# An adaLN transformer block with grouped attention and routed experts on one core: projections and attention rewritten, with unrolled halves, one key tile at a time, and q and k stored once

## The reference

```python
mod = (silu(c) @ wmod).reshape(4, 6, 1, 256)      # sa, ca, ga, sb, cb, gb; |ga|, |gb| at least 0.25
h = layernorm(x) * (1 + ca) + sa                  # x: (4, 512, 256)
q, k, v = h @ wq, h @ wk, h @ wv                  # 32 query heads, 8 key/value heads, head size 8
att = softmax(causal(q @ k.T / sqrt(8)))          # all in float32
x = x + ga * ((att @ v) @ wo)
h = layernorm(x) * (1 + cb) + sb
scores = softmax(h @ gate_w.T)                    # 16 experts in 4 groups; 2 groups, then 4 experts are kept
out = sum over the kept experts of weight * (swiglu(h @ up[e].T) @ down[e].T)
out = out + swiglu(h @ shared_up.T) @ shared_down.T
x = x + gb * out
```

## Time and profile before

| | us |
|---|---|
| median of three unprofiled runs | 829.13 (824.28 to 831.57) |
| span of the profiled execution (its own time; no other is recorded for it) | 853.4 |
| PE busy in it | 669.9 (79%) |
| DVE busy | 472.6 (55%) |
| GpSimd busy | 360.5 (42%) |
| ACT busy | 325.6 (38%) |

### The profile page before, as it was taken

How to read it: one execution, slowest core, us unless ns; L and a number is a source line. 1 busy time by engine, 2 the same in 40 slices (tenths; PEclk the granted TensorE clock), 3 DMA queues, 4 the chain that set the end, 5 groups by cost and what they waited for, 6 DMA issues and landing times.

```text
span 853.4 us, 14386 instructions
## 1 busy us (share of the span) xinstructions
PE 669.9 (79%) x3412; PEld 367.3 (43%) x3413; DVE 472.6 (55%) x921; ACT 325.6 (38%) x752; POOL 360.5 (42%) x441
## 2 busy tenths in 40 slices
PE   1697078999989989998769868435999999999950
PEld 1365033343444444343126436223666566565630
DVE  7496087677859686885357676141333333333326
ACT  1143005675737565573642322011333333333320
POOL 9233114353333534352332574730555455555540
PEclk9999589999999999999677987856999999999995
DMA  5058902141504223220109952332555555555548
GB/s 204 0 168 230 297 26 59 36 120 36 133 21 126 77 70 88 72 77 2 51 3 303 396 153 81 138 136 85 90 90 95 87 96 91 93 89 88 96 49 289
DMA packets 114127, 94.77 MB, mean 111 GB/s; under 512 B 47696, under 2 KB 106032, under 8 KB 114096
## 3 DMA queue, kind: packets, MB, share of 16 engines
q1 hardware_dynamic: 97472, 73.00, 29.4%
q0 software_dynamic: 14448, 19.31, 13.6%
q10 hardware_dynamic: 2176, 2.10, 0.7%
HBM read 47.66 MB, written 44.22 MB: 108 GB/s over the span
## 4 chain that ended last, share of the span: by engine, by line
PE 29%; issue 20%; DVE 12%; DMA 9%; SPq 8%; ACT 5%; POOL 3%; DVEq 1%; POOLq 1%; ACTq 0%
PE bank L812 7%; DMA y_sum<-arena,token_no 7%; PE bank L996 6%; DVE negm L1277 5%; PE bank L802 4%; PE bank L1013 4%; ACT arena L1071 4%; PE bank L784 3%; SPq L724 2%; PE bank L830 2%; DVE arena L544 2%; SPq L725 1%; PE bank L1004 1%; POOL arena L1180 1%; DVE arena L1504 1%
## 5 line engine op out<-in xcount | busy, mean ns | idle before, releaser
L1071 ACT ACTIVATE arena<-bank 128x512 f32<-128x512 f32 x320 | 176.3, 599 | 116.0 <-PE bank L802 112.3
L1277 DVE TENSOR_REDUCE negm<-bank 128x2 f32<-128x1024 f32 (+3 forms) x176 | 190.3, 1116 | 36.8 <-PE bank L788 36.3
L1244 POOL DMA_INDIRECT y_sum<-arena,token_no x79 | 123.0, 1556 | 141.9 <-DVE arena L1509 133.3
L1180 POOL TENSOR_SCALAR_AFFINE_SELECT arena<-arena 128x512 f32<-128x512 f32 x128 | 81.7, 651 | 158.0 <-ACT arena L1071 154.1
L784 PE MATMUL bank<-arena 96*128 96x512 bf16 (+3 forms) x512 | 114.3, 304 | 35.2 <-DVE credits L1263 27.6
L802 PE MATMUL bank<-arena 96*128 96x512 bf16 x320 | 118.7, 400 | 15.4 <-ACT arena L1071 10.8
L996 PE MATMUL bank<-arena 128*128 x316 | 116.2, 491 | 1.1 <-issue 1.1
L1498 DVE CAST token_no<-arena 128x1 uint32<-128x1 f32 x79 | 12.2, 154 | 144.5 <-DMA y_sum<-arena,token_no 133.9
L788 PE MATMUL bank<-mask_qk,ident_bf 128*128 128x128 bf16 (+2 forms) x352 | 87.2, 248 | 0.0
L1235 POOL DMA_INDIRECT x_rows<-arena,slots x64 | 64.2, 1003 | 52.3 <-DVE slots L1410 33.7
L812 PE MATMUL bank<-arena 128*32 128x512 f32 x640 | 79.3, 624 | 6.3 <-POOL arena L1180 6.3
(11 more groups left out here) (174 smaller groups left out, 819.0 us busy)
## 6 DMA issues: line engine op xcount, KB each, us to landing
arena<-x_rows SPq DMA_DIRECT2D x79, 136.5 KB
q_parts<-arena SPq DMA_DIRECT2D x24, 384.0 KB, 3.8
arena<-q_parts SPq DMA_DIRECT2D x32, 288.0 KB
arena<-up_t SPq DMA_DIRECT2D x2, 2816.0 KB
arena<-k_parts SPq DMA_DIRECT2D x16, 288.0 KB
y_parts<-arena SPq DMA_DIRECT2D x64, 64.0 KB
arena<-y_parts SPq DMA_DIRECT2D x16, 256.0 KB, 3.0
arena<-y_sum SPq DMA_DIRECT2D x8, 512.0 KB, 6.9
```

The lines of the kernel that those rows point to most:

```text
L1071: nc.scalar.activation(pool[:, q % 2, g * QT + kt, :], bank[:, buf, :], ACT.Exp, scale=SCALE).then_inc(s["st_free"], 1)
L1180: nc.gpsimd.affine_select(out=block_, in_=block_, compare_op=ALU.is_ge, fill=0.0, base=0, pattern=[[0, REP], [1, P]], channel_multiplier=- ...
L1244: gp.indirect_dma_start(y_sum[i % 2], bass.IndirectOffsetOnAxis(ap=token_no[i % STEPS][:, :], axis=0), yo[i % STEPS], None, compute_op=ALU ...
L1277: nc.vector.tensor_reduce(to, view, AX.X, ALU.max, negate=True).then_inc(s["s_free"], 1)
```

## The change

The two blocks become one, and the halves are written out, u = 0 to 7, with constant counts in all waits. Each part of q and k is stored once (2 stores for each batch), and a load of a half reads them three times, into 24 rows each, for all 512 queries; there are three buffers of `Q` and `K`, and no `K0`. GpSimd clears V and 32 rows of each K, and only behind the first layer norm. PE turns two batches ahead of the projections. The gates are computed once, as 4 rows for the four batches, in the midst of the first maxima, and go through DRAM (`mod_rows`) to all partitions. `GROUPS` orders the score tiles by query tile and key tile, the diagonal one first, and then by g; the exponentials of a group of four go to one of four slots of `probs`, and `weigh_values` runs group by group, where `WEIGH` puts it. The values go out as before, but each total once (`y_totals`); they come back as 128x64, are inverted in one reciprocal, go to DRAM (`y_inverse`) and come back repeated. The last half keeps the old way. The second layer norm starts in the first groups of the last half, the shared expert's weights are loaded ahead of the halves, and the clearing of `y_sum` comes after half 1. Routing, the expert tiles and the end are the same code at other places of `arena`.

```diff
+GROUPS = [(q, kt) for q in range(QT) for kt in (q, *range(q))]
+NG = len(GROUPS)
+E_TOT = NG * GH
+FIRST = {q: GROUPS.index((q, q)) for q in range(QT)}
+S_HEADS = {0: 4, 1: 2, 2: 1, 3: 1}
+S_PAIRS = {q: HH // (2 * S_HEADS[q]) for q in range(QT)}
+S_BASE = {q: sum(S_PAIRS[k] for k in range(q)) for q in range(QT)}
+S_TOT = sum(S_PAIRS.values())
+WEIGH = {1: [(1, 8), (1, 9)], 2: [(0, 0)], 4: [(0, 1), (0, 2)], 6: [(0, 3), (0, 4)], 7: [(0, 5)], 9: [(0, 6), (0, 7)]}
+LEAVE = {1: (1, 3), 2: (0, 0), 4: (0, 1), 7: (0, 2)}
+SLOTS = 4
+QBUF = 3
...
-    q_parts = nc.dram_tensor("q_parts", (B, 2, PARTS, PARTS, HD, HH, T), BF16, kind="Internal").ap()
-    k_parts = nc.dram_tensor("k_parts", (B, 2, PARTS, PARTS, HD, GH, T), BF16, kind="Internal").ap()
+    q_parts = nc.dram_tensor("q_parts", (B, 2, PARTS, HD, HH * T), BF16, kind="Internal").ap()
+    k_parts = nc.dram_tensor("k_parts", (B, PARTS, 2, HD, GH * T), BF16, kind="Internal").ap()
...
-                for h in range(2):
-                    nc.gpsimd.memset(Q[h][:, :, :, :], 0.0)
-                    nc.gpsimd.memset(K[h][:, :, :], 1.0)
-                    last = nc.gpsimd.memset(K0[h][:, :, :], 0.0)
-                last.then_inc(s["cleared_q"], 1)
...
+        def pairs_after(q, slot):
+            n = (q + 1) * GH
+            return range(slot * S_PAIRS[q] // n, (slot + 1) * S_PAIRS[q] // n)
...
+                def store_parts(b):
+                    i = b % 2
+                    sp.wait_ge(s["low_done"], b + 1)
+                    sp.dma_start(q_parts[b].rearrange("h j d (n t) -> (d n) (h j) t", n=HH),
+                                 parts[i][:, 0:2, :, :].rearrange("p h j t -> p (h j) t")).then_inc(q_out[i], 16)
+                    sp.dma_start(k_parts[b].rearrange("j h d (g t) -> (h d g) j t", g=GH),
+                                 parts[i][0:64, 2, :, :]).then_inc(q_out[i], 16)
+                def load_half(u):
+                    b, h, i = u // 2, u % 2, u % QBUF
+                    for n in range(PARTS):
+                        rows_ = slice(PARTS * HD * n, PARTS * HD * n + PARTS * HD)
+                        sp.dma_start(Q[i][rows_, :, :].rearrange("p n t -> p (n t)"),
+                                     q_parts[b, h].rearrange("j d m -> (j d) m")).then_inc(q_in[i], 16)
+                        sp.dma_start(K[i][rows_, :, :].rearrange("p g t -> p (g t)"),
+                                     k_parts[b, n, h].unsqueeze(0).to_broadcast([PARTS, HD, GH * T])).then_inc(k_in[i], 16)
...
+                def fetch_values(u):
+                    h = u % 2
+                    sp.wait_ge(y_out[h], 128 * (u // 2 + 1))
+                    above(sp, s["y_ready"], u)
+                    if u % 2 == 0:
+                        above(sp, s["x2_ready"], u)
+                    sp.dma_start(totals, y_totals[h].rearrange("n (a t) -> (n a) t", a=P // (GH * REP))).then_inc(t_in[h], 16)
+                    sp.dma_start(Yp[0][:, :], y_values[h].rearrange("g r d t -> (g r d) t")).then_inc(y_in[h], 16)
+                def spread_inverse(u):
+                    h = u % 2
+                    sp.wait_ge(s["inverted"], u + 1)
+                    sp.dma_start(y_inverse[h].rearrange("n (a t) -> (n a) t", a=P // (GH * REP)), inverse
+                                 ).then_inc(i_out[h], 16)
+                    sp.wait_ge(i_out[h], 16 * (u // 2 + 1))
+                    sp.dma_start(Yp[1][:, :], y_inverse[h].unsqueeze(1).to_broadcast([GH * REP, HD, T])).then_inc(y_in[h], 16)
...
+                store_parts(0)
+                store_parts(1)
+                sp.wait_ge(q_out[0], 32)
+                sp.wait_ge(s["k_ones"], QBUF)
+                load_half(0)
+                load_half(1)
+                store_parts(2)
+                store_parts(3)
+                sp.wait_ge(q_out[1], 32)
+                load_half(2)
+                sp.wait_ge(s["gate_rows"], 1)
+                sp.dma_start(mod_rows, row_mod[0:B, :, :].rearrange("p m d -> p (m d)")).then_inc(s["gate_out"], 16)
+                sp.wait_ge(s["gate_out"], 16)
+                sp.dma_start(gate_bc[:, :, :, :].rearrange("p b m d -> p (b m d)"),
+                             mod_rows.rearrange("b m -> (b m)").unsqueeze(0).to_broadcast([P, B * 4 * D])
+                             ).then_inc(s["gate_bc"], 16)
...
+                for u in range(HALVES):
+                    if u > 0 and u + 2 < HALVES:
+                        sp.wait_ge(s["st_ready"], E_TOT * u)
+                        if (u + 2) % 2 == 0:
+                            sp.wait_ge(q_out[(u // 2 + 1) % 2], 32 * ((u // 2 + 1) // 2 + 1))
+                        load_half(u + 2)
+                    put_negm(u, QT - 1)
+                    if u > 0:
+                        send_values(u - 1)
+                    if u + 1 < HALVES:
+                        put_negm(u + 1, 0)
+                    if u > 0:
+                        fetch_values(u - 1)
+                    if u + 1 < HALVES:
+                        put_negm(u + 1, 1)
+                    if u > 0:
+                        spread_inverse(u - 1)
+                    if u + 1 < HALVES:
+                        put_negm(u + 1, 2)
...
+                def gate_rows():
+                    pe.wait_ge(s["wg_in"], 16)
+                    for k in range(2):
+                        for c in range(DC):
+                            last = nc.tensor.matmul(bank[0:B, 6 + k, :], sc_sb[:, c, :],
+                                                    wmod_sb[:, c, GA * P + 512 * k:GA * P + 512 * k + 512],
+                                                    start=(c == 0), stop=(c == DC - 1))
+                    last.then_inc(s["gate_mm"], 1)
...
+                def weigh_values(u, n):
+                    b, h, (q, kt) = u // 2, u % 2, GROUPS[n]
+                    pe.wait_ge(s["st_free"], E_TOT * u + GH * n + GH)
+                    if kt == q:
+                        pe.wait_ge(s["p_ready"], GH * (QT * u + q) + GH)
+                        above(pe, s["o_free"], QT * u + q)
+                    for g in range(GH):
+                        last = nc.tensor.matmul(bank[32 * g:32 * g + 32, OBANK, :], V[:, b * QT + kt, h * GH + g, :],
+                                                probs[:, (NG * u + n) % SLOTS, g, :], start=(kt == q),
+                                                stop=(kt == max(q - 1, 0)), skip_group_check=True)
                     last.then_inc(s["av_done"], 1)
...
+                            slot = GH * (n - FIRST[q]) + g
+                            scores(u, n, g)
+                            if g == 0:
+                                for back_, m in WEIGH.get(n, ()):
+                                    if u - back_ >= 0:
+                                        weigh_values(u - back_, m)
+                            if u + 1 < HALVES:
+                                for i in pairs_after(q, slot):
+                                    scores_for_max(u + 1, q, i)
+                            if (n, g) == (0, 2):
+                                turn_max(u, QT - 1)
+                            elif kt == q and g == 2 and u + 1 < HALVES:
+                                turn_max(u + 1, q - 1)
+                            if u % 2 == 0 and u > 0 and (n, g) in ((8, 3), (9, 1)):
+                                project(u // 2 - 1, int(n == 9))
...
+                turn_x(0)
+                turn_x(1)
+                pe.wait_ge(s["w_in"], 48)
+                for b in range(B):
+                    project_in(b)
+                    if b + 2 < B:
+                        turn_x(b + 2)
...
+                    if q == 1:
+                        gate_rows()
+                        pe.wait_ge(s["gate_rows"], 1)
...
+                            tile = E_TOT * u + GH * n + g
+                            act.wait_ge(s["st_ready"], tile + 1)
+                            nc.scalar.activation(probs[:, group % SLOTS, g, :], bank[:, 4 + tile % 2, :], ACT.Exp,
+                                                 scale=SCALE).then_inc(s["st_free"], 1)
+                        if u == HALVES - 1 and n == FIRST[QT - 1]:
+                            deviation2(act, 0, B - 1)
...
+                gp.wait_ge(s["xn_ready"], 1)
+                nc.gpsimd.memset(V, 1.0).then_inc(s["v_ones"], 1)
+                gp.wait_ge(s["v_ones"], 1)
+                for i in range(QBUF):
+                    nc.gpsimd.memset(K[i][64:96, :, :], 1.0).then_inc(s["k_ones"], 1)
+                    gp.wait_ge(s["k_ones"], i + 1)
+                low(0)
...
+                def invert(u):
+                    dve.wait_ge(t_in[u % 2], 16 * (u // 2 + 1))
+                    nc.vector.reciprocal(inverse, totals).then_inc(s["inverted"], 1)
+                def normalise(u):
+                    dve.wait_ge(y_in[u % 2], 32 * (u // 2 + 1))
+                    nc.vector.tensor_tensor(Y[u % 2][:, :], Yp[0][:, :], Yp[1][:, :], ALU.mult).then_inc(s["y_ready"], 1)
...
```

(9 more changed lines are left out.)

993 lines of the change are left out of this document (425 added, 568 removed).

## The result

The changed kernel takes 802.9 us (median of 4 runs, 799.3 to 806.2) where the kernel before, run beside it, takes 830.4 (824.3 to 832.8): ratio 0.9694, 95% interval 0.9641 to 0.9747. It is faster by 27 us; 71 were forecast, and the time lies outside my range. The profiled execution took 799.3 us.

What follows compares the result with a forecast made beforehand. It took the head as bound by clearing and SyncE's serial stores and loads, the halves by DVE behind at q = 3 with PE stalling. Head -43, halves -19, last half -9 sum to -71: 829.1 - 71 = 758 us, range 730 to 788.

Steps and rivals of the forecast that it cites:

- Head: Everything up to the first half's E scores: earlier projections, fewer stores, gates moved; -43 us, from -30 to -50.
- (a): Head: GpSimd clears less, behind the first layer norm; projections start near 18.5 instead of 31.34: -13 us.
- (b): Head: gate matmuls, 3.62 to 3.72 us a batch, leave the projection loop; projections end near 54, was 80.
- (c): Head: fewer stores, first half's data loaded in 5.5 us; first scores near 57 instead of 107.5: -50, between -35 and -55.
- the rule on K's load: Head: K's load, its source repeated 3 times, uses 3 engines: 5.6 us, hidden, or scores 2 to 3 later.
- Step (d): First maxima: gates as rows, PE 3.6 then DVE near 4; +5 us, between 0 and 9; broadcast ends near 81.
- Halves: Attention halves: odd 34, even 38 us, with up to 2 us stall for totals; -19 us, from -5 to -38.
- DVE's 3 us: In each half: one 128x64 reciprocal replaces four of 128x128, 3.5 us becoming about 0.5, -3 on DVE.
- Last half: Last half: early second norm, 36 us to the end of scores instead of 41.4, fewer values behind; -9, 0 to -14.
- Rival (1): Only the head pays; halves bound by PE alternating with ACT and DVE, and by late totals: 781 us, chance 0.17.
- Rival (4): Head gains only 25: 16 KB rows at half rate, loads ahead of later stores and gates; 776 us, chance 0.12.
- Rival (3): Unrolled halves: straight code stalls about 11.5 us in each of 8, 92 in all; 850 us, chance 0.03.

Runs made afterwards that it cites:

- k_rows: The changed kernel with rows of q and k in the order (dimension, part), so K's load has no leading repeat of 3: 776.8 us, ratio 0.9386.
- k_split: The changed kernel with each load of K split into three loads of 8 rows without a repeat, in the old order: ratio 0.9508.
- before_again: The kernel before, unchanged, profiled a second time: span 830.0, time 831.8 us.
- gates_first: The changed kernel with the third half's load behind the gates' rows, their broadcast and the first three minus-max rows in SyncE's queue: 803.6 us, ratio 0.9666.
- invert_late: The changed kernel with DVE's reciprocal of the totals three tiles later in the half: 788.8 us, ratio 0.9505.
- recip_small: The kernel before with each reciprocal on 16 of 128 columns, leaving out part of the result: 826.6 us, ratio 0.9949.
- recip_big: k_rows with twelve more reciprocals of 128x32 a half on DVE: 795.9 us, ratio 0.9624.
- bridge_last: k_rows with gates earlier, third half's load and reciprocal later, and unused matmuls in the last half, ten before the square-root wait: 768.4 us, ratio 0.9276.
- all_six: bridge_last with 22 unused matmuls ahead of the first scores: 765.0 us, ratio 0.9239.
- k_rows_again: k_rows, unchanged, measured again as a reference: 779.0 us, ratio 0.9415.

## Why the prediction was wrong, step by step

**Head, -43 forecast, -28 to -31 measured.** Steps (a), (b) and the stores of (c) held: projections from 19.95 (18.5 forecast) to 53.1 (54), stores at 36.7 and 45.2 (36 and 45), DVE's first `tensor_scalar` 1.38. The term that failed is "the data of the first half at 275 GB/s takes 5.5": the first scores came at 68.1 instead of 57, and 8.0 us of the 11 are the load of K, as k_rows shows and k_split confirms (62.3, with Q's load untouched). The other 3 remain in k_rows (60.1); the wait of 7.16 there is still for K. I had put the rule on K's load into a sentence of its own, with 2 to 3 us estimated by the Trainium skill ("DMA: Bandwidth & Descriptors", section on why a DMA increments its semaphore by 16). Its sign held: with 8 as the slowest dimension the load is faster than with 3, in both forms tried. My price from it was too small, 8.0 at the first scores, and it left out the queue behind the load; no row here shows how many engines a load took. Step (d), the gates, was +5 and is 7.25 (76.05 to 83.30), PE's 3.6 and DVE's 3.6 one behind the other; and the maxima run at a granted clock of 0.50 from 83.3 on. First scores to first E takes 35.2 where 24.4 + 5 were reckoned; the 24.4 came from one trace at a clock of 0.92, and in before_again the same stretch takes 26.7 at 0.63. The broadcast of the gates does not "end near 81": it starts at 95.1, behind the third half's load, and that cost only the 1.2 us wait (gates_first).

**Halves, -19 forecast, 0 measured.** The step that failed is "up to 2 us of stall, of which the two banks of scores cover half". The place was nearly right (the totals come back 17.8 to 19.2 us behind the half's turn where DVE waits for them, and in k_rows the reciprocal runs at 17.4) and so was the size: DVE waits 0.3 to 1.73 us. But the three waits over 1 us were not covered: PE waits 1.35 to 1.80, and behind two of them its clock fell for 7 us. Two things were left out: that the load of the half after next stands ahead of the totals in SyncE's queue, so that their last store took 8.4 us to land where I had 2 to 3 for a crossing, and that a short wait can cost more than its length. With the stall gone (invert_late, k_rows) the halves are 35.0 and 38.6, forecast 34 and 38, together -12 of the 19; the first half gained nothing by turns (36.9 against 36.4 and 35.9), at a clock of 0.84 where the kernel before has 0.95 to 1.00; that the clock is the whole reason was not tested. The mechanism I gave for it, DVE's 3 us, holds only in half: alone it gives 2 to 4 us in seven halves (recip_small), while the new order with 4 us given back to DVE loses 16 (recip_big). What the tile order and the spread values give by themselves was not tried apart from the unrolling.

**Last half, -9 forecast, -1 to -2 measured.** The early norm 2 took the wait of 3.65 us for ACT away from one place, and the square root made one of 2.4 in another. I took 36 us for PE at the low level with nothing waiting, where PE and ACT in fact take turns: 33.3 busy of 43.4. With unused matmuls in the gaps, and the clock at 0.96 and 1.00, bridge_last and all_six take 39.4 and 37.7 us. The failed term is this 36 without a wait, and part of the miss is luck of the draw: k_rows_again takes 38.9 with no fill, 4.5 us less than k_rows.

**Rivals.** Rival (1), "only the head pays", is what happened, by one of the two mechanisms it named for the halves, the late totals; the other, the alternation of PE with ACT and DVE through two banks, is not what held them, since they fell to 34.9 and 38.4 in invert_late with both pairs of banks as they were. Rival (4) was right on the head, by another load than the one it blamed (it had 16 KB rows of Q; it was K), and in its order of events: stores of batch 2 and 3 late, gates behind. By their own terms together they are 829 - 25 - 0 - 5 = 799; measured are 829 - 28 - 0 - 1 = 800. I had given them 0.17 and 0.12 as if they excluded each other, and the range reached only over each alone, although both hang on the same queue. Rival (3), stalls of straight code: the waits of ACT without a releaser stand in the looped kernel and in variants of the unrolled one, and not in other traces of either, so the code does not decide them; in the unrolled halves there is none, which agrees with the Trainium skill ("Runtime: NRT & Kernel Launch", section on instruction fetch).

## What to carry to other kernels

A transfer is priced with what stands behind it in its queue: list for each queue what waits for a later entry, and see whether loads with time to spare can stand behind small transfers that an engine waits for (in the head this gave 1.2 us, gates_first; in the halves it was not tried, but the one without a load ahead had no wait). Look at the slowest dimension of both sides of a transfer; a row order without a repeat of 3 there was worth 26 us of 803 and cost nothing to change. When an engine's work is shortened but its operand now makes a round trip, move the operation to where the operand surely is, since two waits of 1.35 and 1.80 us on the way to TensorE cost over 4 each, and a third of 1.70 only itself. Before a stretch is compared between two kernels, look at how far it moves between two traces of one: the last half here took 43.4 and 38.9. Rivals that share a cause should be summed in the range.
